# Second scan stage of a fused two-layer network: three front steps one place later, the first pair weights ahead of the loads

## What is computed

```python
x = x + _L1_attn_a_ref(_layernorm(x, axis=-1), ...)

delta = jax.nn.softplus(x @ W_delta + b_delta)
Bm = x @ W_B
Cm = x @ W_C
A = -jnp.exp(A_log)
def step(h, inp):
    x_t, d_t, B_t, C_t = inp
    bar_A = jnp.exp(jnp.minimum(d_t[..., None] * A, 10.0))
    bar_B = jnp.clip(d_t[..., None] * B_t[:, None, :], -10.0, 10.0)
    h = jnp.clip(bar_A * h + bar_B * x_t[..., None], -10000.0, 10000.0)
    y_t = jnp.sum(h * C_t[:, None, :], axis=-1) + x_t * D_param
    return (h, y_t)
...
flat = ssm_out.reshape(-1, D)
probs = jax.nn.softmax(flat @ W_router, axis=-1)     # 4 experts, top 2, follow
```

## Time and profile before

| | us |
|---|---|
| median of three runs | 4913.53 |
| lowest and highest run | 4904.8 and 4913.81 |
| the profiled execution, its own time | 4910.68 |
| its span in the profile | 4908.9 |
| the second scan stage in it: lead-in | about 2303 to 2360 |
| its loop | about 2364 to 2846 |

### The profile page before, as it was taken

The page is one execution under the profiler, slowest core; times in us unless marked ns, Lnnn a source line. Parts: engine busy times, 40 slices in busy tenths (PEclk is TensorE's granted clock), DMA queues, the critical chain, the costliest instruction groups (busy, mean ns, idle before and its releaser), DMA issues.

```text
span 4908.9 us, 49219 instructions
## 1 busy us (share of the span) xinstructions
PE 3882.5 (79%) x15176; PEld 2243.6 (46%) x15178; DVE 2842.9 (58%) x4909; ACT 2210.7 (45%) x4071; POOL 2466.1 (50%) x2147
## 2 busy tenths in 40 slices
PE   6788888759956888797788869986875798888892
PEld 2333333347743556576334336654662233334571
DVE  5999999951126675211689952227333677664522
ACT  5665666521127775111566533333343355555241
POOL 5999999922212234211799944432455412222256
PEclk9999999959978999898789979996986699998896
DMA  5555655522210010221455521124156323321144
GB/s 154 159 160 162 160 155 160 154 72 75 101 54 17 18 35 27 96 95 63 136 162 159 150 92 45 45 71 125 57 151 129 108 41 45 45 32 55 39 141 132
DMA packets 311640, 476.06 MB, mean 97 GB/s; under 512 B 34762, under 2 KB 167606, under 8 KB 311306
## 3 DMA queue, kind: packets, MB, share of 16 engines
q1 hardware_dynamic: 276864, 388.61, 29.1%
q0 software_dynamic: 28992, 75.72, 5.4%
q10 hardware_dynamic: 5504, 8.39, 0.6%
HBM read 374.87 MB, written 97.10 MB: 96 GB/s over the span
## 4 chain that ended last, share of the span: by engine, by line
PE 37%; DVE 8%; issue 4%; ACT 4%; POOL 4%; DMA 3%; SPq 0%; DVEq 0%; ACTq 0%; POOLq 0%
PE s_gate_up L2325 8%; PE s_result_sum L2341 4%; PE s_hidden_sum L1761 3%; PE s_result_sum L1772 3%; PE s_out_sum L3696 3%; PE s_shared L2981 2%; PE s_scores L3637 2%; PE s_scores_T L3680 2%; DVE s_maxima L3328 2%; DVE s_decay L370 2%; PE s_shared L2991 1%; POOL s_gathered L1047 1%; PE s_transposed L2315 1%; PE s_mid_transposed L2334 1%; DVE s_h L377 1%
## 5 line engine op out<-in xcount | busy, mean ns | idle before, releaser
L435 POOL TENSOR_TENSOR s_h<-s_dtu,s_bc 128x1024 f32<-128x1024 f32 x384 | 902.5, 2359 | 48.9 <-PE s_y_sum L477 37.1
L477 PE MATMUL s_y_sum<-s_h,identity 128*128 128x512 f32 x1536 | 763.9, 635 | 133.4 <-POOL s_h L444 121.2
L402 ACT ACTIVATE s_decay<-s_dt,s_A 128x512 f32<-128x512 f32 x768 | 498.4, 682 | 309.1 <-DVE s_h L377 302.1
L477 PEld LDWEIGHTS s_y_sum<-s_h,identity 128*128 128x128 f32 x1536 | 292.8, 201 | 570.5 <-issue 291.0
L2325 PE MATMUL s_gate_up<-s_w_gate_up,s_rowsT 128*128 x1168 | 414.8, 487 | 1.7 <-issue 1.5
L3502 ACT ACTIVATE s_weights_T<-s_scores_T 128x1024 f32<-128x1024 f32 (+3 forms) x384 | 292.6, 811 | 260.0 <-PE s_scores_T L3680 258.3
L3328 DVE TENSOR_REDUCE s_maxima<-s_scores 128x1 f32<-128x512 f32 (+3 forms) x463 | 296.5, 658 | 187.2 <-PE s_scores L3641 104.3
L444 POOL TENSOR_TENSOR s_h<-s_h,s_bc 128x512 f32<-128x512 f32 x288 | 365.8, 1271 | 17.1 <-DVE s_h L370 12.4
L2384 DVE TENSOR_TENSOR s_mid<-s_act,s_gate_up 128x128 f32<-128x128 f32 (+1 forms) x225 | 91.5, 407 | 445.7 <-ACT s_act L2357 445.7
L3550 POOL TENSOR_SCALAR_AFFINE_SELECT s_weights_T<-s_weights_T 128x256 f32<-128x256 f32 x256 | 102.7, 406 | 472.2 <-ACT s_weights_T L3502 469.5
L370 DVE TENSOR_TENSOR_SCAN s_decay<-s_decay,s_carry,s_h 128x512 f32<-128x512 f32 x240 | 302.7, 1275 | 15.8 <-ACT s_decay L402 11.5
(11 more groups left out here) (533 smaller groups left out, 7644.7 us busy)
## 6 DMA issues: line engine op xcount, KB each, us to landing
s_bc<-s_bc_rows SPq DMA_DIRECT2D x384, 512.0 KB, 5.2
sorted_results<-s_result SPq DMA_DIRECT2D x158, 128.0 KB, 2.2
s_w_inter<-in_L_ffn_experts_inter SPq DMA_DIRECT2D x16, 1024.0 KB, 5.0
s_w_exp_out<-in_L_ffn_experts_out SPq DMA_DIRECT2D x16, 1024.0 KB, 7.9
s_queries<-parts_of_q SPq DMA_DIRECT2D x96, 128.0 KB, 4.9
s_keys<-parts_of_k SPq DMA_DIRECT2D x96, 128.0 KB, 8.0
results_by_token<-zeros SPq DMA_DIRECT2D x16, 512.0 KB, 5.9
s_pair<-results_by_token SPq DMA_DIRECT2D x16, 512.0 KB
```

Source lines behind the costliest of these rows:

```text
L402: S.e.activation(self.decay[:, (2 * g + d) % 4, :], dt[q // self.passes % 2][:, at, :], ACT.Exp, scale=A[:, at, g % ns:g % ns + 1]).then_i ...
L435: G.e.tensor_tensor(self.h[r][:], dtu[q // self.passes % 2][:, at:at + 2, :], mid(self.bc[r][:, 0, :], 2), ALU.mult).then_inc(*self.fed.up())
L477: made = T.e.matmul(self.y[:, d, :], ident[:], self.h[r][:, d, :], start=False, stop=g % ns == ns - 1)
```

## The change

It has two parts. In the lead-in ScalarE makes the pair weights of chunk 0 before it waits for the stage's loads, and TensorE's waits for those loads and for ScalarE's diagonals move from the start of its program to the transposes of `front`. VectorE's own wait for the loads is dropped; its wait for ScalarE's exponential stays. In the loop the B and C products and their copy, the delta products, and the logits products and their copy get ticks later by one.

```diff
     def vector():
-        V.wait_ge(*loaded.now())
         V.wait_ge(*a_exp.at(0))
...
     def scalar():
+        pairs.scalar_weights(0)
         S.wait_ge(*loaded.now())
         S.e.activation(A[:], A[:], ACT.Exp).then_inc(*a_exp.up())
...
             yield 1
-            pairs.scalar_weights(c)
+            if c > 0:
+                pairs.scalar_weights(c)
...
-            yield 13
+            yield 14
             S.wait_ge(*bc_made.at(c))
             S.wait_ge(*sc.stored.at(c - 1))
             S.wait_ge(*rows_read.at(c - 1))
...
-            yield 28
+            yield 29
             S.wait_ge(*logit_made.at(c))
...
             yield 9
             T.wait_ge(*ln.used.at(c))
+            T.wait_ge(*loaded.now())
+            T.wait_ge(*a_exp.at(1))
             banks_free()
...
-            yield 12
+            yield 13
             banks_free()
...
             made.then_inc(*bc_made.up())
             free[0] = rows_made.at(c)
-            yield 15
+            yield 16
             banks_free()
             T.wait_ge(*a_ready.at(1))
...
-            yield 27
+            yield 28
             T.wait_ge(*free[1])
...
-        T.wait_ge(*loaded.now())
-        T.wait_ge(*a_exp.at(1))
         sc.tensor(skip, xT, x_made, early=early, front=front, back=back)
```

## The result

The kernel after took 4919.2 us (median of 13 runs, 4907.5 to 4929.74), the kernel before beside it 4908.88 us (13 runs, 4900.9 to 4916.91): ratio 1.002, 95% interval 1.0011 to 1.0029, so slower by some 10 us (5 to 14). Forecast were 3 us less. Measured again on another chip, the same kernel came out at 1.0007 (0.9994 to 1.0020), which doesn't tell it from the kernel before. So the size of the loss is uncertain in the whole time; the traces say more.

A forecast was written before the change was run, and what follows sets the result against it. A serial chain was taken to bound the lead-in, GpSimd (93% busy) and VectorE (90%) together the loop. -6.0 + 3.5 - 0.5 = -3.0 us took the median from 4913.53 to 4910.5; range 4900 to 4920.

The forecast's parts named there:

- Part 1, the lead-in: Stage's lead-in: pair weights made early, so the pair sum starts at 2308.6, 6.0 us earlier (bounds 3.4 and 6.6).
- Part 2, VectorE's stall: Loop: VectorE's row maximum waits for the later rows copy, 0.8 or 1.1 us a chunk; 3.5 us stay.
- delta waits for the copy as well: Loop, read in c1: delta starts at 2459.7 and not 2458.85, behind ScalarE's later copy of B and C.
- the 0.9 us that I wrote off: Loop, TensorE: unit 6 summed about 0.9 us earlier; delta's wait for the copy takes most of it back.
- the hiding places: Idle time in c0 and c2 and ScalarE's wait in c6 hide the stall there; otherwise 3.3 us more.
- Part 3, the logits: Chunk ends: statistics products precede the logits, at no cost; in c7 the last sums come 0.5 us earlier.
- hidden by 2 us: Chunk end: unit 12, summed 2 us later, is done at 2488.5, before GpSimd's feed at 2490.59 needs it.
- Ring slots held back: Rival, loop: unit 12's late sum holds GpSimd's feed of the next chunk; +14.8 us, 4928.3; chance 0.06.
- All stalls count: Rival, loop: c0, c2 and c6 hide nothing, stalls cost 6.8 us; in all +0.3, 4913.8; chance 0.17.
- Relief of GpSimd: Rival, loop: GpSimd sets the pace, stalls are hidden, 6.3 us come off; in all -12.9, 4900.6; chance 0.11.
- The lead-in does not do what it says: Rival, lead-in: halves land with the eight loads, gaining only 3.4 us; in all -0.4, 4913.1; chance 0.11.
- the waits of GpSimd for TensorE above 18 us: Loop: a listed sign that the forecast is wrong; before, GpSimd waited 18.2 us for TensorE's sums.

The follow-up runs named there:

- b3_stat_behind_logits: The kernel after with TensorE's statistics product of the last unit moved back behind the logits: loop 485.7 us, lead-in 48.8, ratio to before 0.9992.
- a3_bc_delta_only: The kernel before with TensorE's B and C and delta products and ScalarE's rows copy one place later: loop 488.4 us, ratio to before 1.0007.
- a1_lead_only: The kernel before with the new lead-in alone, all ticks as before: lead-in 50.8 us, loop 482.0, ratio to before 0.9988.
- b1_rows_copy_back: The kernel after with ScalarE's copy of the B and C rows back in its old place: loop 485.5 us, ratio to before 0.9987.
- a2_loop_only: The kernel before with all five later ticks of the loop and the old lead-in: loop 494.2 us, ratio to before 1.0017.
- e1_after_again: The kernel after unchanged, measured once more on another chip: loop 493.5 us, lead-in 51.2, ratio to before 1.0007.
- a4_logits_only: The kernel before with only the logits product and its copy one place later, behind the statistics: loop 482.9 us, ratio to before 1.0009.
- b4_pe_bc_only: The kernel before with only TensorE's B and C and delta products one place later: loop 479.9 us, ratio to before 0.9997.

## Why the prediction was wrong, step by step

**Part 1, the lead-in, -6.0: right in its mechanism, the size off in both terms.** The landing of the halves is what is late next, as written, but it comes 6.3 us after the first load's issue, not 5.2 (5.7 to 6.3 over the ten traces with the new lead-in); the gain from it is 4.9 us. The estimate of 4.4 us from the second issue, 2303.8, was earlier still than mine (the Trainium skill, DMA: Bandwidth & Descriptors, Anatomy of one DMA): in after it took 5.9 us, so the trace does not bear it out for two halves with eight more loads behind them. The other 4.8 us are TensorE's clock, which I had taken as the same "in both orders": the pair sum took 5.29 us and not 6.33, and delta of c0 took 7.7 us and not 11.5, since its second half ran at full clock (1.98 and 1.12 us), which in the trace of before it never did. This is luck of an execution in part: the lead-in ran from 48.8 to 55.9 us with the new order and from 56.9 to 61.1 with the old.

**Part 2, VectorE's stall, +3.5: the stall right, the step "delta waits for the copy as well" mis-sized.** The stall was forecast at 0.8 and 1.1 us, some 6.8 in all; it is 0.68 and 0.94, 5.8 in all. Delta's wait was taken as 0.85 us from c1, where TensorE came late to it because its B and C product had taken 3.28 us; that is the slow speed. In c3 of the kernel before the same product took 1.90 us, and TensorE was at delta at 2579.93 while the decays ran to 2581.83. With the copy's 0.59 us behind them, these rows would have given a wait of 2.5 us:

```profile
2575.41 1.90 PE L2683 MATMUL s_front<-s_xT,s_w_bc 128*32 128x512 f32 x4 [1.73 <-ACT s_xT L2583]
2577.25 2.84 PE L477 MATMUL s_y_sum<-s_h,identity 128*128 128x512 f32 x6
2579.93 1.88 PE L2691 MATMUL s_front<-s_xT,s_w_delta 128*128 128x512 f32 x4
...
2580.53 1.30 ACT L402 ACTIVATE s_decay<-s_dt,s_A 128x512 f32<-128x512 f32 x2 [2.00 <-DVE s_h L377]
```

(Timelines of TensorE and ScalarE in c3 of the kernel before.) One chunk stood for seven, and it was the one that hid the wait. Nor had the prediction a term for the clock that may fall behind it, which costs 1.2 us in c0, 2.7 in c3 and 2.7 in c5 of after, read from VectorE's waits for `dt`. TensorE's earlier product, the 0.9 us that I wrote off, gives 2.6 us by itself, mostly in c2 and c6 (61.6 to 60.8 and 58.7 to 56.5). In c6 that is more than a product: B and C took 3.62 us at half clock in both old loops and 1.90 in all four with the new place. And of the hiding places only c0 can have hidden something. Against TensorE's front alone, c0 of b3_stat_behind_logits is longer by 0.3 us, and the wait at c1's first scan falls from 1.7 to 0.7. But c6 is longer by 1.0 there and c2 by 1.1 in a3_bc_delta_only, and the six chunks of a3_bc_delta_only without a fall of the clock are longer by 3.8 us for 4.2 us of stalls. The idle time at c3's first scan does fall from 1.31 to 0.26 us, but it does so without any stall. Two errors cancelled here by luck: 5.8 less 2.6 is 3.2, and my term was 3.5.

**Part 3, the logits, -0.5: the failed step.** The 2 us of lateness were "hidden by 2 us" behind GpSimd's feed at 2490.59. In after GpSimd did wait there for only 0.89 us. I had asked who waits for unit 12 and not who waits for the last sum: ScalarE's copy of `y_sum`, which went without a wait at 2495.06, holds the pair weights and decays behind it. In five chunks of the kernel after (c2 to c6) it waits 1.05 to 2.61 us, and in c2 to c5 VectorE's scan of unit 3 waits 2.08 to 2.93 us where it had 0.24 to 1.26. The working also added old durations after an idle time that had grown to 5.97 us; behind it the one product ahead of the logits took 2.08 us and not 0.89. The gain in c7 came, with 1.5 us in after where I took 0.5.

**The sum.** VectorE was busy for the same time, so its waits tell where the loop's 14.1 us went. The stall at the rows is +5.8. The waits for `dt` are +5.1. At unit 3's scans it waits 10.9 us in all where it had 3.9: +7.0. The other way go the waits at the chunks' first scans (3.9 to 1.7, -2.2) and the end, from the last scan to the last copy of `y_sum` (4.7 to 3.3, -1.5). Together that is 14.2. Built up from the experiments instead: the old loop takes 482.3 us (mean of before and a1_lead_only), TensorE's front gives -2.6, VectorE's stall costs +6.0 (b3_stat_behind_logits, which has one fall of the clock in it) and the late statistics +5.8 (b1_rows_copy_back): 491.5. What is left to the measured 496.8, 494.2 and 493.5 goes by the clock: how often it fell ahead of delta (in c0, c3 and c5 of after and of a2_loop_only, in c0 and c5 of e1_after_again), and in how many chunks it stayed low behind the statistics. Such a sum can't be exact, since a part's cost depends on what stands beside it.

**The interaction.** The late statistics cost 5.8 us over TensorE's new front and 0.0 to 0.5 over the old one. Chunk by chunk, b1_rows_copy_back is longer than the front alone by 2.4 us in c2, 0.8 in c3, 0.5 in c4 and 3.3 in c5; a4_logits_only is longer than before by 2.0 in c2 and shorter by 1.4 in c6. The relief in c6, B and C at full clock, is one that the new front gives as well, and it can't come twice. In the other chunks the copy of `y_sum` is late where TensorE's clock stays low behind its idle time ahead of the statistics. Two stretches from the statistics to that copy, both from c4, b1_rows_copy_back first and then a4_logits_only (columns as above):

```profile
2665.96:2681.80 15.84, 15.80 (x38) 8.35 (x38) 15.84 (x18) 6.31 (x14) 13.87 (x14) 0.60 0.53 142
2674.79:2687.38 12.59, 11.22 (x38) 5.71 (x38) 12.59 (x15) 6.16 (x15) 12.21 (x13) 0.87 0.57 155
```

The idle time ahead of them is 5.61 and 6.05 us, the copy waits 3.19 us and not at all. It is so throughout: of the 42 such stretches (c1 to c6 in the seven traces with the statistics ahead of the logits) 27 have a mean granted clock of 0.60 to 0.67, and the copy waits 1.0 to 3.2 us in each; the other 15 have 0.85 to 0.89, and it never waits. What isn't settled is why the clock comes back sooner in one chunk than in another, nor why the same idle time of 2.31 us ahead of delta is followed by half clock in one chunk and not in another.

**The rivals.** "Ring slots held back" had the right sign, and its condition, TensorE at its lower clock behind the statistics, came true, but its reader was the wrong one: what held VectorE up was the copy of `y_sum`, not the feed. "All stalls count" was right on VectorE's stall. "Relief of GpSimd" had the part that b4_pe_bc_only shows. "The lead-in does not do what it says" did not come true: in after the pair sum started 1.5 us before the last load had landed. Of the signs listed, the waits of GpSimd for TensorE above 18 us (34.4) were the one that told it was wrong, and it told so by a wait that VectorE didn't feel.

**Still open.** The stage grew by 4.4 and 1.2 us in the two traces of after, the whole kernel by 10 (5 to 14) and 3.4 (-3 to +10). No trace shows a loss elsewhere: what comes behind the stage took 2062.0 us before and 2055.2 and 2051.5 after. Scatter of the unchanged code can hold the difference; it is not shown to.

## What to carry to other kernels

When an instruction moves on one engine, walk to the next reader of everything that gets late with it, in order, and not to the one reader that was found first; on an engine that works in order, what counts is what is queued behind that reader. Read the slack in several repetitions of a loop, above all in those where the engine ran at its fast speed, since a slow one hides a wait that the move will open. And test the steps of a moved group apart: here one of three gained (2.6 us), one was neutral by itself and cost 5.8 beside the first, one cost 6 to 9, and the new lead-in with the gaining step alone is the fastest version (ratio to before 0.9974, twice).

## What the runs showed of the hardware

- Behind the same idle time TensorE's granted clock can fall from 1.00 to 0.50 (2.4 to 1.2 GHz) or hold: 2.30 us in c5 of b3_stat_behind_logits were followed by full clock (delta 6.0 us), 2.31 us in c5 of a3_bc_delta_only by half (9.3 us), and in both TensorE had idled 2.57 us ahead of B and C as well. In the six traces with such waits the clock fell in 12 of the 24 chunks where TensorE waited 1.97 to 2.31 us ahead of delta. It fell after TensorE had started again: in c3 of after it was still 1.00 through the wait and 0.58 in the mean of the 8 us behind it.
- Behind an idle time of 4.6 to 6.3 us ahead of the statistics the mean clock up to the next copy of `y_sum` was either 0.60 to 0.67 or 0.85 to 0.89, and only in the first case did that copy wait.
- The same program gave a lead-in of 55.9 and of 51.2 us. The Trainium skill (TensorE: Matmul & The Clock Gate, Part 1) says that the window by which the chip judges TensorE runs freely and doesn't start with the kernel, so that the point of change varies from run to run. The traces fit that, with delta of c0 in 11.5 us in the one and 7.8 in the other; they don't show the window itself.
- 1.05 MB in two transfers issued first, with eight more loads behind them, were there 5.7 to 6.3 us after the first issue; the last of the ten had landed 7.3 to 8.8 us after it, over both orders.
